# Projections of an attention layer computed feature-major: q and k leave TensorE transposed, the bias is added on VectorE

## The chip, the cores and the metric

The kernel runs on one core of a Trainium2 chip. The metric is the device time of one launch in microseconds. Before the change three runs took 682.51, 686.03 and 685.92 us, median 685.92. The engines are called PE (TensorE, matmul), DVE (VectorE), ACT (ScalarE), POOL (GpSimd) and SP (SyncE, which issues all DMAs here). Each runs its own program in order; they meet by semaphores.

## The reference

Eight sequences of 512 tokens with 256 features, 16 heads of 16. A cross-attention with rotary position, then a feed-forward part with fake quantisation, each behind a gate:

```python
q, k, v = proj(layernorm(x), Wq, bq), proj(ctx, Wk, bk), proj(ctx, Wv, bv)
q = q * cos + rotate_half(q) * sin          # the same for k
attn_w = softmax(q k^T / 4)
x = x + tanh(g0) * ((attn_w v) Wo + bo)
s = sigmoid(clip_x) * max|xn| / 127;  xq = clip(round(xn / s)) * s      # xn = layernorm(x)
h = fake_quant(silu(xq Wg) * (xq Wu), clip_down)     # weights quantised by row
x = x + tanh(g1) * (h Wd)
```

Everything is float32. The scores are computed from three bfloat16 parts of q and k (high, middle, low; six products), so they keep about the accuracy of float32.

## The kernel before

There are three blocks, and all engines leave one together before they enter the next.

**Projection block** (`psA`). It goes through 32 tiles of 128 tokens, four to a batch (a sequence). For a tile, DVE normalises x (`x_normalise`), PE transposes it (`pe_tile`, L256), and multiplies with tokens stationary and weights moving: `v_ps` (L266, 256 columns), the bias of q and k as a bfloat16 matmul of a ones tile with three bias parts (L272, 512 columns), k (L274) and q (L280). DVE rotates q and k out of PSUM with three tensor_tensor (L337 to L339), POOL adds the two halves (L356), PE transposes the result in four pieces (L289), ACT makes the high part from PSUM (L311), DVE the rest from PSUM (L346), ACT the middle part (L305), POOL the low part (L360). The parts go to a scratch tensor in HBM, half a batch at a time (`store`, L369), because the attention wants them by head. `ctx` has two buffers of half a batch, loaded from HBM when the projection of the half before is done (L387). DVE also takes the moments of the next batch (`statistics`, `ln_moments`, L157), POOL the power (-0.5) for them (`ln_power`, L163), and DVE, in the fourth tile of a batch, the largest values of the feed-forward weights (`wmax`, L467), with scales and reciprocals (`winv`) in the last batch. SP loads unit 0 (12 DMAs, `load_unit`, L184) during batch 6 and unit 1 during batch 7, six after each half.

**Attention block** (`psB`). 32 units of four heads. PE computes, two units ahead, the scores by query (`query_scores`, L669), of which DVE takes the row maxima (`maxima`, L880); POOL splits the maxima in two bfloat16 parts (`split_max`, L1004), PE transposes them (`max_transpose`, L694, in step 0 of the unit before the one they serve), ACT copies them (`take_max`), and SP puts them in the q tile as two rows (L628). Then PE computes the scores by key (`scores`, L660), ACT the exponential (L833), PE the weighing of v (`weigh`, L682). A unit has four steps (`kt`), in each 4 maxima on DVE. At its start POOL quantises the gate and up weights with `winv` (L1047, 12 instructions) before batch 0; between batch 0 and batch 1 it makes `woT`, `diag`, the quantised down weights and the integer copy `wfq` (L1050 to L1057).

**Feed-forward block** (`psC`). Not touched by the change.

## Time and profile before

| | us |
|---|---|
| median of three runs | 685.92 |
| the profiled execution | 683.17 |
| its span, first to last instruction | 681.4 |
| PE busy | 613.5 (90%) |
| DVE busy | 569.2 (84%) |
| ACT busy | 432.0 (63%) |
| POOL busy | 249.5 (37%) |
| mean granted clock of PE, share of full | 0.972 |

Busy shares are means over blocks with different limits: the projection block ends at about 143 us, attention at about 580 us. In the rows below, "x4" is a count of instructions merged in one row; a float32 matmul is recorded as two. Times of matmuls include the way through the array, so two that follow each other overlap in the records; the distance between starts is the cost. "[1.96 <-DMA ctx]" is idle time of the engine before the row and what ended it.

### The profile page before, as it was taken

The numbers are of one execution on the slowest core, as the hardware profiler recorded it, in microseconds if no ns is written. First come the engines' busy times: TensorE is split into PE (matmuls) and PEld (weight loads), VectorE is DVE, ScalarE is ACT, GpSimd is POOL, SyncE is SP. The second block draws the span as 40 slices with busy tenths as digits, with TensorE's granted clock in tenths as the row PEclk, the third lists the DMA queues.
The fourth block names the chain that finished last, engine by engine and source line by source line (L and its number), as shares of the span: only waits on it lengthen the run. The fifth ranks groups of instructions, "written<-read, shape, count | busy, mean of one in ns | idle before, by whom it ended". The sixth has DMA issues, their size and how long they took to land. (4 is left out here: it accounts for less than half of the span.)

```text
span 681.4 us, 19413 instructions
## 1 busy us (share of the span) xinstructions
PE 613.5 (90%) x6569; PEld 324.2 (48%) x6574; DVE 569.2 (84%) x1052; ACT 432.0 (63%) x822; POOL 249.5 (37%) x357
## 2 busy tenths in 40 slices
PE   1999998878999999999999999999999997478675
PEld 1777777742544444444444444444444444233254
DVE  7788888878899888888888888988988935489878
ACT  1344544431778776776777777777767774388694
...
GB/s 248 103 176 177 175 180 154 182 140 97 43 68 83 53 69 71 52 66 70 50 69 68 48 68 70 47 66 73 48 67 74 4 1 1 0 1 0 1 62 185
DMA packets 74922, 54.71 MB, mean 80 GB/s; under 512 B 10755, under 2 KB 74371, under 8 KB 74886
## 3 DMA queue, kind: packets, MB, share of 16 engines
...
q14 instruction: 15, 0.12, 0.1%
...
## 5 line engine op out<-in xcount | busy, mean ns | idle before, releaser
L880 DVE TENSOR_REDUCE negm<-mx_ps 128x1 f32<-128x512 f32 x512 | 322.1, 684 | 42.2 <-PE mx_ps L669 37.8
L833 ACT ACTIVATE prob<-st_ps 128x512 f32<-128x512 f32 x512 | 279.2, 600 | 112.7 <-PE st_ps L660 109.9
L669 PE MATMUL mx_ps<-k,q 96*32 96x512 bf16 x2048 | 209.0, 392 | 6.1 <-DVE negm L880 4.9
L660 PE MATMUL st_ps<-q,k 98*32 98x512 bf16 x2048 | 204.0, 385 | 0.2
L682 PE MATMUL pv_ps<-prob,v_u 128*32 128x512 f32 x1024 | 133.4, 592 | 0.3 <-ACT oT L846 0.2
L669 PEld LDWEIGHTS mx_ps<-k,q 96*32 96x32 bf16 x2048 | 56.9, 97 | 103.3 <-DVE negm L880 68.8
L660 PEld LDWEIGHTS st_ps<-q,k 98*32 98x32 bf16 x2048 | 57.9, 96 | 79.6 <-ACT prob L833 34.4
L1004 POOL TENSOR_TENSOR msplit<-negm,onesf 128x16 bf16<-128x16 f32 x32 | 7.1, 221 | 239.2 <-DVE negm L880 234.7
L356 POOL TENSOR_TENSOR qk<-rc,rs 128x512 f32<-128x512 f32 x32 | 40.7, 1271 | 35.0 <-DVE rs L339 35.0
L311 ACT ACTIVATE part<-qkT_ps 128x512 bf16<-128x512 f32 x32 | 19.1, 597 | 42.0 <-PE qkT_ps L289 42.0
L360 POOL TENSOR_TENSOR part<-r,part 128x512 bf16<-128x512 f32 x32 | 38.2, 1194 | 11.9 <-ACT part L305 11.8
L266 PE MATMUL v_ps<-wkv,ctx 128*128 128x256 f32 x128 | 35.5, 402 | 6.4 <-DMA ctx<-in_ctxT 6.4
L682 PEld LDWEIGHTS pv_ps<-prob,v_u 128*32 128x32 f32 x1024 | 32.6, 110 | 18.1 <-issue 1.0
L337 DVE TENSOR_TENSOR rc<-qk_ps,rope_t 128x512 f32<-128x512 f32 x32 | 22.1, 690 | 21.4 <-PE qk_ps L280 18.6
L1247 ACT ACTIVATE wf<-banks,gscale 128x512 f32<-128x512 f32 x44 | 30.0, 696 | 10.6 <-PE banks L1204 4.2
L1394 POOL TENSOR_TENSOR hst<-hq_even,wf 128x512 f32<-128x512 f32 x24 | 30.8, 1302 | 15.5 <-ACT hq_even L1253 15.2
L274 PE MATMUL qk_ps<-wkv,ctx 128*128 128x256 f32 x128 | 33.7, 386 | 0.0
L280 PE MATMUL qk_ps<-wq,xnT 128*128 128x256 f32 x128 | 33.7, 387 | 0.0
L1014 POOL COPY v_u<-V 128x256 f32 (+1 forms) x32 | 12.7, 396 | 49.9 <-PE pv_ps L682 49.8
L1208 PE MATMUL banks<-wfq,wgT 128*128 128x512 bf16 x77 | 23.9, 390 | 4.9 <-ACT wf L1247 3.1
L274 PEld LDWEIGHTS qk_ps<-wkv,ctx 128*128 128x128 f32 x128 | 24.9, 194 | 6.7 <-issue 0.3
L764 PE MATMUL misc_ps<-woT,attnT 128*128 128x256 f32 x112 | 27.8, 391 | 0.0
...
## 6 DMA issues: line engine op xcount, KB each, us to landing
...
q<-mrow SPq DMA_DIRECT2D x64, 4.0 KB, 2.7
...
```

The lines of the kernel that those rows point to most:

```text
L266: last = nc.tensor.matmul(v_ps[r][:, 0:D], ctx[hf][:, c, at:at + P], wkv[:, c, D:2 * D], start=(c == 0), stop=(c == KC - 1))
L274: nc.tensor.matmul(qk_ps[r][:, D:2 * D], ctx[hf][:, c, at:at + P], wkv[:, c, 0:D], start=False, stop=(c == KC - 1), skip_group_check=True)
L280: last = nc.tensor.matmul(qk_ps[r][:, 0:D], xnT[r][:, c, :], wq[:, c, :], start=False, stop=(c == KC - 1), skip_group_check=True)
L356: nc.gpsimd.tensor_tensor(qk[q][:], rc[q][:], rs[q][:], ALU.add).then_inc(roped, 1)
L360: nc.gpsimd.tensor_tensor(parts[j // 2][2][:, :, (j % 2) * P:(j % 2 + 1) * P], r1[i % 2][:], parts[j // 2][1][:, :, (j % 2) * P:(j % 2 + 1 ...
L660: last = nc.tensor.matmul(st_ps[bank(i)][lo:lo + COLS, :], k6[g][:, h, kt * P + lo:kt * P + lo + COLS], q6[g][:, h, :], start=True, stop=True)
L669: last = nc.tensor.matmul(mx_ps[bank(i)][lo:lo + COLS, :], q6[g][0:ROWS, h, qt * P + lo:qt * P + lo + COLS], k6[g][0:ROWS, h, :], start=Tr ...
L682: last = nc.tensor.matmul(pv_ps[32 * h:32 * h + 32, :], v_u[g % 2][:, kt, h, :], prob[kt % 2][:, h, :], start=(kt == 0), stop=(kt == TPB - 1))
L833: nc.scalar.activation(prob[kt % 2][:, h, :], st_ps[bank(HPU * kt + h)][:], ACT.Exp, scale=SCALE).then_inc(exp_done, 1)
L880: nc.vector.tensor_reduce(negm[g % 2][:, h * TPB + qt:h * TPB + qt + 1], mx_ps[bank(TPB * h + qt)][:], op=ALU.max, axis=AX.X, negate=True) ...
L1247: nc.scalar.activation(sil[s % UR], g_ps[s % GR], ACT.Silu, scale=gscale[:, c:c + 1]).then_inc(sil_ready, 1)
L1394: nc.gpsimd.tensor_tensor(hst[:, bass.ds(SLOTS * p + s, 1), :].rearrange("p o t -> p (o t)"), upb[j % UBR], sil[s % UR], ALU.mult).then_in ...
```

## The change

A batch is handled as a whole. PE holds a 128x128 piece of the weights and moves 512 tokens: k (4 matmuls of 512 columns), the 8 transposes of the normalised x, v (tokens stationary, as before), q (4 of 512 columns). q and k come out with features on partitions, in the order "first halves of all heads, second halves of all heads" (the weights are reordered on the host), so a rotation is two scalar_tensor_tensor on DVE for each quarter i (k first half, k second half, q first half, q second half) that add the bias, with a sum or difference after it. The four transposes of q and k and the bias matmul are gone. ACT normalises x instead of DVE. The rotation table grows from 64 KB to 512 KB. The weight maxima go to batch 0 of the attention block, and with them the gate and up quantisation on POOL goes behind batch 0. The SP loop of the projection block is unrolled, and the other engines peel two batches.

```diff
-parts = [[sb(mid, f"part{n}_{i}", [P, 4, 2 * P], BF16) for n in range(3)] for i in range(2)]
+parts = sb(mid, "parts", [P, 4, 3, S], BF16)
-rope_t = sb(mid, "rope_t", [P, TPB, 2, HD])
+work = sb(mid, "work", [P, 4, 2, S])
+bias = sb(mid, "bias", [P, 4])
+cs = sb(mid, "cs", [P, 2, S])
-ctx = [sb(stA, f"ctx{i}", [P, KC, 2 * P]) for i in range(2)]
+ctx = sb(stA, "ctx", [P, KC, S])
+xn = sb(stA, "xn", [P, TPB, D])
+xnT = sb(stA, "xnT", [P, KC, S])
+xT_ps = ps(psA, "xT_ps", [P, KC, S])
+q_ps = ps(psA, "q_ps", [P, 2, S])
+v_ps = ps(psA, "v_ps", [P, TPB, D])
+k_ps = ps(psA, "k_ps", [P, 2, S])
...
+def rope(dve, b, i):
+    h = i % 2
+    dve.wait_ge(qk_ready, 2 * b + i // 2 + 1)
+    if not is_first(b):
+        dve.wait_ge(lo_ready, 4 * (b - 1) + i + 1)
+    src = (k_ps, q_ps)[i // 2]
+    nc.vector.scalar_tensor_tensor(work[:, i, 0, :], src[:, h, :], bias[:, i:i + 1], cs[:, 0, :], ALU.add, ALU.mult)
+    o = i + 1 - 2 * h
+    nc.vector.scalar_tensor_tensor(work[:, i, 1, :], src[:, 1 - h, :], bias[:, o:o + 1], cs[:, 1, :], ALU.add, ALU.mult).then_inc(rot_ready, 1)
+def rope_sum(eng, ns, b, i):
+    eng.wait_ge(rot_ready, 4 * b + i + 1)
+    ns.tensor_tensor(work[:, i, 0, :], work[:, i, 0, :], work[:, i, 1, :], ALU.add if i % 2 else ALU.subtract)\
+        .then_inc(roped_last if i == 3 else roped, 1)
+def hi_part(act, b, i):
+    if i == 3:
+        act.wait_ge(roped_last, b + 1)
+    else:
+        act.wait_ge(roped, 3 * b + i + 1)
+    if not is_first(b):
+        act.wait_ge(stored[i], NSTORE * b)
+    nc.scalar.activation(parts[:, i, 0, :], work[:, i, 0, :], ACT.Copy).then_inc(hi_ready, 1)
+def rest_part(dve, b, i):
+    dve.wait_ge(hi_ready, 4 * b + i + 1)
+    nc.vector.tensor_tensor(work[:, i, 1, :], work[:, i, 0, :], parts[:, i, 0, :], ALU.subtract).then_inc(r1_ready, 1)
+def mid_part(act, b, i):
+    act.wait_ge(r1_ready, 4 * b + i + 1)
+    nc.scalar.activation(parts[:, i, 1, :], work[:, i, 1, :], ACT.Copy).then_inc(mid_ready, 1)
+def lo_part(pool, b, i):
+    pool.wait_ge(mid_ready, 4 * b + i + 1)
+    nc.gpsimd.tensor_tensor(parts[:, i, 2, :], work[:, i, 1, :], parts[:, i, 1, :], ALU.subtract).then_inc(lo_ready, 1)
+scr_rows = scratch.rearrange("n (w c) f t -> n w (c f) t", w=2).rearrange("n w (h e d) t -> n w e h d t", e=2, d=HD // 2)
+def store(sp, b, i):
+    sp.wait_ge(lo_ready, 4 * b + i + 1)
     for n in range(3):
-        sp.dma_start(scr_v[n, :, :, bass.ds(b * S + hf * 2 * P, 2 * P)], parts[hf][n][:]).then_inc(stored[hf], DMA)
+        sp.dma_start(scr_rows[n, 1 - i // 2, i % 2, :, :, bass.ds(b * S, S)], parts[:, i, n, :]).then_inc(stored[i], DMA)
...
+        def load_ctx(b, hf):
+            at = hf * 2 * P
+            if not is_first(b):
+                sp.wait_ge(v_ready, 2 * (b - 1) + hf + 1)
+            sp.dma_start(ctx[:, :, at:at + 2 * P], ctx_v[:, :, bass.ds(b * S + at, 2 * P)]).then_inc(ctx_in[hf], DMA)
         def body(b, unit=None):
+            for i in range(3):
+                store(sp, b - 1, i)
+            if not is_last(b):
+                for hf in range(2):
+                    load_ctx(b + 1, hf)
+            store(sp, b - 1, 3)
+            if unit is not None:
+                load_unit(sp, 0, unit)
+            else:
+                sp.wait_ge(x_in, DMA * (b + 1))
+                load_x(b + 2, x_in)
...
+                pe.wait_ge(ctx_in[hf], DMA * (b + 1))
+            if is_first(b):
+                pe.wait_ge(k_in, DMA)
+            else:
+                pe.wait_ge(rot_ready, 4 * (b - 1) + 2)
+            for m in range(2):
+                for c in range(KC):
+                    last = nc.tensor.matmul(k_ps[:, m, :], wk[:, c, m * P:(m + 1) * P], ctx[:, c, :], start=(c == 0), stop=(c == KC - 1))
+            last.then_inc(qk_ready, 1)
...
+                pe.wait_ge(const_ready, CONSTS)
+            pe.wait_ge(xn_ready, TPB * (b + 1))
+            for c in range(KC):
+                if not is_first(b):
+                    pe.wait_ge(xnT_ready, KC * (b - 1) + c + 1)
+                for t in range(TPB):
+                    last = nc.tensor.transpose(xT_ps[:, c, t * P:(t + 1) * P], xn[:, t, c * P:(c + 1) * P], ident[:])
+                last.then_inc(xT_ready, 1)
+            if is_first(b):
+                pe.wait_ge(v_in, DMA)
+            for j in range(2):
+                if not is_first(b):
+                    pe.wait_ge(v_kept, 2 * (b - 1) + j + 1)
+                for t in (2 * j, 2 * j + 1):
+                    for c in range(KC):
+                        last = nc.tensor.matmul(v_ps[:, t, :], ctx[:, c, t * P:(t + 1) * P], wv[:, c, :], start=(c == 0), stop=(c == KC - 1))
+                last.then_inc(v_ready, 1)
+            if is_first(b):
+                pe.wait_ge(q_in, DMA)
+            else:
+                pe.wait_ge(rot_ready, 4 * (b - 1) + 4)
+            for m in range(2):
+                for c in range(KC):
+                    if m == 0:
+                        pe.wait_ge(xnT_ready, KC * b + c + 1)
+                    last = nc.tensor.matmul(q_ps[:, m, :], wq[:, c, m * P:(m + 1) * P], xnT[:, c, :], start=(c == 0), stop=(c == KC - 1))
+            last.then_inc(qk_ready, 1)
...
+        def normalise(b):
+            act.wait_ge(shift_ready, b + 1)
+            wait_if(act, xT_ready, KC * b)
+            for t in range(TPB):
+                T = TPB * b + t
+                nc.scalar.activation(xn[:, t, :], X[:, bass.ds(T, 1), :].rearrange("p o d -> p (o d)"), ACT.Identity,
+                                     bias=shift[:, bass.ds(T, 1)], scale=rstd[:, bass.ds(T, 1)]).then_inc(xn_ready, 1)
         def body(b):
+            if not is_first(b):
+                for i in (0, 1):
+                    mid_part(act, b - 1, i)
+                for i in (2, 3):
+                    hi_part(act, b - 1, i)
+            for c in range(KC):
+                act.wait_ge(xT_ready, KC * b + c + 1)
+                if c == 0:
+                    wait_if(act, qk_ready, 2 * b)
+                nc.scalar.activation(xnT[:, c, :], xT_ps[:, c, :], ACT.Copy).then_inc(xnT_ready, 1)
+            if not is_first(b):
+                for i in (2, 3):
+                    mid_part(act, b - 1, i)
+            for j in range(2):
+                act.wait_ge(v_ready, 2 * b + j + 1)
+                nc.scalar.activation(V[:, bass.ds(TPB * b + 2 * j, 2), :], v_ps[:, 2 * j:2 * j + 2, :], ACT.Copy).then_inc(v_kept, 1)
+            for i in (0, 1):
+                hi_part(act, b, i)
+            if not is_last(b):
+                normalise(b + 1)
+        normalise(0)
+        over_batches(act, body, B, True, 2)
...
+            ahead = not is_last(b)
+            if not is_first(b):
+                for i in (2, 3):
+                    rope(dve, b - 1, i)
+            if ahead:
+                dve.wait_ge(x_in, DMA * (b + 1))
+                statistics(b + 1, (0, 1))
+            if not is_first(b):
+                rope_sum(dve, nc.vector, b - 1, 3)
+            if ahead:
+                statistics(b + 1, (2, 3))
+            if not is_first(b):
+                for i in (2, 3):
+                    rest_part(dve, b - 1, i)
+            for i in (0, 1):
+                rope(dve, b, i)
+            if ahead:
+                dve.wait_ge(ln_ready[0], b + 1)
+                ln_moments(nc.vector, dve, 0, b + 1)
+            for i in (0, 1):
+                rest_part(dve, b, i)
 ...
+        def scale_and_shift(b):
+            ln_power(pool, 0, b)
+            pool.wait_ge(ln_ready[0], b + 1)
+            cols = bass.ds(TPB * b, TPB)
+            nc.gpsimd.tensor_tensor(shift[:, cols], negmean[:, cols], rstd[:, cols], ALU.mult).then_inc(shift_ready, 1)
         def body(b):
+            if not is_first(b):
+                lo_part(pool, b - 1, 0)
+                rope_sum(pool, nc.gpsimd, b - 1, 2)
+                lo_part(pool, b - 1, 1)
+                lo_part(pool, b - 1, 2)
+            rope_sum(pool, nc.gpsimd, b, 0)
+            if not is_first(b):
+                lo_part(pool, b - 1, 3)
+            rope_sum(pool, nc.gpsimd, b, 1)
+            if not is_last(b):
+                scale_and_shift(b + 1)
...
+                    if is_first(b):
+                        weight_maxima(TPB * g + kt)
...
+        def weight_maxima(n):
+            if n == 0:
+                dve.wait_ge(late_in, 11 * DMA)
+            if n < 12:
+                nc.vector.tensor_reduce(wmax[:, n:n + 1], wf[:, n, :], op=ALU.max, axis=AX.X, apply_absolute_value=True).then_inc(w_step, 1)
+            elif n < 12 + KC:
+                i = n - 12
+                nc.vector.tensor_reduce(wmax[:, WD + i:WD + i + 1], wd[:, i, 0:INNER], op=ALU.max, axis=AX.X,
+                                        apply_absolute_value=True).then_inc(w_step, 1)
+            elif n == 14:
+                dve.wait_ge(w_step, 2 * NIC + KC)
+                for lo, hi in ((0, 2 * NIC), (WD, NROW)):
+                    last = nc.vector.tensor_scalar(wscale[:, lo:hi], wmax[:, lo:hi], 1.0 / QMAX, None, ALU.mult)
+                last.then_inc(w_step, 1)
+                dve.wait_ge(tanh_ready, 2)
+                nc.vector.tensor_scalar(clips[:], clipe[:], 1.0, QMAX, ALU.add, ALU.mult).then_inc(clip_step, 1)
+            else:
+                dve.wait_ge(w_step, 2 * NIC + KC + 1)
+                for lo, hi in ((0, 2 * NIC), (WD, NROW)):
+                    last = nc.vector.reciprocal(winv[:, lo:hi], wscale[:, lo:hi])
+                last.then_inc(w_step, 1)
+                dve.wait_ge(clip_step, 1)
+                nc.vector.reciprocal(clips[:], clips[:])
...
+        pool.wait_ge(bo_ready, 2)
+        body(0)
+        pool.wait_ge(w_step, 2 * NIC + KC + 2)
         for i in range(2 * NIC):
             nc.gpsimd.tensor_scalar(wf[:, i, :], wf[:, i, :], winv[:, i:i + 1], MAGIC, ALU.mult, ALU.add)
-        pool.wait_ge(bo_ready, 2)
-        body(0)
```

At the start SP loads, in order, wk, both halves of ctx, x of batch 0, the bias, the rotation table, wv, wq, x of batch 1, the gates, ctx and x of later batches, and the feed-forward weights. In the attention block the parts of batch 7 that are left are made between the first maxima (DVE: `rope` 2 and 3, four maxima, `rope_sum` 3, four maxima, `rest_part` 2 and 3).

## Rows read from the trace of the kernel before

**Rows 1.** Timeline of SP's DMA issues: start, us, engine, line.
```profile
48.89 1.53 SPq L369 DMA_DIRECT2D qk_parts<-part  x3
...
110.55 1.53 SPq L369 DMA_DIRECT2D qk_parts<-part  x3
...
112.13 3.40 SPq L184 DMA_DIRECT2D k<-qk_parts  x6
...
115.58 0.43 SPq L387 DMA_DIRECT2D ctx<-in_ctxT  x1
```

**Rows 2.** Timeline of PE, one tile, and one wait for ctx.
```profile
111.40 0.38 PE L272 MATMUL qk_ps<-b_parts,onesb 96*128 96x512 bf16 x1
...
111.62 1.03 PE L274 MATMUL qk_ps<-wkv,ctx 128*128 128x256 f32 x4
...
113.35 0.60 PE L289 MATMUL qkT_ps<-ident,qk 128*128 128x128 f32 x4
...
113.78 0.38 PE L256 MATMUL xT_ps<-ident,xn 128*128 128x128 f32 x2
...
114.87 0.38 PE L272 MATMUL qk_ps<-b_parts,onesb 96*128 96x512 bf16 x1
...
119.60 1.13 PE L266 MATMUL v_ps<-wkv,ctx 128*128 128x256 f32 x4 [1.96 <-DMA ctx<-in_ctxT]
```

**Rows 3.** Busy time by stretch: us; PE, PEld, DVE, ACT, POOL; granted clock.
```profile
180.00:191.00 11.00, 11.00 (x165) 5.76 (x165) 10.00 (x17) 8.76 (x18) 0.84 (x4) 1.00 0.31 76
```

**Rows 4.** Groups by form, first 115 us: busy us, mean ns, idle before.
```profile
L356 POOL TENSOR_TENSOR qk<-rc,rs 128x512 f32<-128x512 f32 x25 | 31.8, 1272 | 28.0 <-DVE rs L339 28.0
...
L360 POOL TENSOR_TENSOR part<-r,part 128x512 bf16<-128x512 f32 x23 | 27.7, 1203 | 4.2 <-ACT part L305 4.2
...
L346 DVE TENSOR_TENSOR r<-qkT_ps,part 128x512 f32<-128x512 f32 x24 | 16.4, 682 | 0.2 <-issue 0.2
...
L467 DVE TENSOR_REDUCE wmax<-wf x5 | 3.4, 678 | 0.0
...
L163 POOL TENSOR_TENSOR rstd<-ln_tmp,ln_const 128x4 f32 x5 | 5.6, 1116 | 1.9 <-DVE ln_tmp L157 1.9
```

**Rows 5.** Groups by form after 590 us (feed-forward part).
```profile
L1320 DVE SCALAR_TENSOR_TENSOR hst<-banks,gscale,wf 128x512 f32<-128x512 f32 x10 | 7.5, 746 | 8.8 <-ACT wf L1247 8.7
```

**Rows 6.** Timeline of ACT in the attention part.
```profile
217.95 2.73 ACT L833 ACTIVATE prob<-st_ps 128x512 f32<-128x512 f32 x5
```

**Rows 7.** One line's instructions: duration ns min/median/max.
```profile
L157 DVE TENSOR_TENSOR ln_tmp<-stats x21: 150/153/1149, 26.1 to 119.7; 128x4 f32 x18, 128x4 f32<-128x4 f32 x3
```

**Rows 8.** Timeline: both engines in one such place.
```profile
118.45 1.26 POOL L356 TENSOR_TENSOR qk<-rc,rs 128x512 f32<-128x512 f32 x1 [0.96 <-DVE rs L339]
...
118.88 1.00 DVE L157 TENSOR_TENSOR ln_tmp<-stats 128x4 f32 x3
```

**Rows 9.** Timeline of the first microseconds: POOL's memset of the k tiles.
```profile
8.01 7.61 POOL L534 MEMSET k<- 2x2048 bf16 x4
```

**Rows 10.** Timeline across the end of the projection block.
```profile
143.87 0.69 DVE L337 TENSOR_TENSOR rc<-qk_ps,rope_t 128x512 f32<-128x512 f32 x1 [2.71 <-PEq L373]
```

**Rows 11.** Timeline of POOL in the attention part, first batch.
```profile
158.14 5.46 POOL L1047 TENSOR_SCALAR wf<-wf,winv 128x256 f32<-128x256 f32 x12
...
204.78 1.04 POOL L1050 TENSOR_TENSOR woT<-wo_raw,tanhg 128x512 f32<-128x512 f32 x1
...
208.38 4.03 POOL L1057 TENSOR_SCALAR wfq<-wf 128x4608 bf16<-128x4608 f32 x1
...
213.57 0.22 POOL L1004 TENSOR_TENSOR msplit<-negm,onesf 128x16 bf16<-128x16 f32 x1 [1.16 <-DVE negm L880]
```

**Rows 12.** Timeline of PE there.
```profile
215.88 0.23 PE L694 MATMUL misc_ps<-identb,msplit 128*32 128x128 bf16 x1
```

**Rows 13.** Busy time by stretch, end of attention, same columns as rows 3.
```profile
580.00:583.00 3.00, 0.00 (x0) 0.00 (x0) 2.00 (x5) 0.00 (x0) 0.93 (x1) 0.83 0.00 0
...
589.00:592.00 3.00, 2.77 (x7) 1.06 (x7) 0.00 (x0) 1.18 (x2) 0.00 (x0) 0.50 0.00 0
```

More of the change, by code:

```diff
@@ L55, with over_batches @@
 DMA = 16
-def over_batches(eng, body, count, peel_last):
-    body(0)
-    with eng.Fori(1, count - 1 if peel_last else count) as b:
+def over_batches(eng, body, count, peel_last, peel_first=1):
+    for b in range(peel_first):
+        body(b)
+    with eng.Fori(peel_first, count - 1 if peel_last else count) as b:
         body(b)
@@ L102, in build @@
         mean = sb(top, "mean", [P, NT])
+        negmean = sb(top, "negmean", [P, NT])
+        shift = sb(top, "shift", [P, NT])
         rstd = sb(top, "rstd", [P, NT])
@@ L141, in ln_moments @@
             cols = bass.ds(TPB * b, TPB)
-            half, quarter, per, eps, _ = (ln_const[:, i, :] for i in range(len(LN_CONST)))
+            half, quarter, per, eps, neg_half = (ln_const[:, i, :] for i in range(len(LN_CONST)))
             levels = [[(tmp[0][:], stats[:, cols, 1], stats[:, cols, 4], ALU.add),
@@ L154, in ln_moments @@
                 if done:
-                    eng.wait_ge(step, LN_STEPS * b + done)
+                    eng.wait_ge(step, LN_STEPS[k] * b + done)
                 for out, x0, x1, op in level:
@@ L240, in build @@
         lo_ready = sem("lo_ready")
[L241 removed]
+        stored = [sem(f"stored{i}") for i in range(4)]
         NSTORE = 3 * DMA
[L244 to L290 removed]
@@ L373, in build @@
+        CONSTS = 5
         with nc.Block() as block:
@@ L396, in _ @@
+                sp.dma_start(wk[:], a["wkT"].rearrange("(c p) n -> p c n", p=P)).then_inc(k_in, DMA)
+                for hf in range(2):
+                    load_ctx(0, hf)
                 load_x(0, x0_in)
-                sp.wait_ge(b_zero, 1)
-                sp.dma_start(b_raw[0:65:32, :], a["bqk"].partition_broadcast(3)).then_inc(bias_in, DMA)
-                sp.dma_start(wkv[:], a["wkvT"].rearrange("(c p) n -> p c n", p=P)).then_inc(kv_in, DMA)
-                sp.dma_start(ctx[0][:], ctx_v[:, :, 0:2 * P]).then_inc(ctx_in[0], DMA)
+                sp.dma_start(bias[:], a["bkq"]).then_inc(bias_in, DMA)
@@ L405, in _ @@
                 sp.dma_start(gates[:], a["gates"].partition_broadcast(P)).then_inc(gate_in, DMA)
-                body(0)
+                for hf in range(2):
+                    load_ctx(1, hf)
                 sp.wait_ge(x_in, DMA)
@@ L419, in _ @@
                 sp.dma_start(bv_col[:], a["bv_col"]).then_inc(late_in, DMA)
-                with sp.Fori(1, B - 2) as b:
+                for b in range(1, B - 2):
                     body(b)
-                for hf in range(2):
-                    sp.wait_ge(stored[hf], NSTORE)
+                for i in range(4):
+                    sp.wait_ge(stored[i], NSTORE)
                 body(B - 2, 0)
@@ L489, in _ @@
+                    for i in (0, 1):
[5 more added lines that the diff above has]
+                        rest_part(dve, b, i)
                 dve.wait_ge(ln_const_ready, len(LN_CONST))
                 dve.wait_ge(x0_in, DMA)
-                for i in range(2):
-                    statistics(0, i)
+                statistics(0, range(TPB))
@@ L512, in _ @@
-                body(B - 1)
+                dve.wait_ge(bias_in, 2 * DMA)
+                over_batches(dve, body, B, True, 2)
             @block.gpsimd
             def _(pool):
-                def body(b):
-                    for i in range(TPB):
-                        pool_tile(pool, TPB * b + i, i, 0)
-                        if i == 2 and not is_last(b):
-                            ln_power(pool, 0, b + 1)
-                nc.gpsimd.memset(b_raw[:], 0.0).then_inc(b_zero, 1)
+                def scale_and_shift(b):
[3 more added lines that the diff above has]
+                    nc.gpsimd.tensor_tensor(shift[:, cols], negmean[:, cols], rstd[:, cols], ALU.mult).then_inc(shift_ready, 1)
```

277 lines of the change are left out of this document (48 added, 229 removed).

## The prediction, made before the changed kernel was run

> **What bounds the kernel now.** I read the slices first (TensorE is full from about 170 us to 570 us and ragged before), then the timeline of each stage, then the groups by form for durations.
>
> The projection block (to about 143 us). SP stores the first half of a batch at 48.89 and four batches later at 110.55 [rows 1]: 61.66 / 4 = 15.4 us a batch. On PE a tile takes 114.87 - 111.40 = 3.47 us without a gap, four tiles 13.9 us, and the rest is the wait for `ctx`: issued at 115.58, used at 119.60, PE idle 1.96 us [rows 1, 2]. So this block is TensorE plus a late reload. The other engines have room: POOL has 1.27 + 1.20 us a tile plus 1.1 us a batch [rows 4], 11.0 us of 15.4.
>
> The attention block. A unit takes about 11 us in its first batch, PE 11.00 of 11.00 us, DVE 10.00 [rows 3]. PE is the bound with DVE close behind. A PE stall there is not given back.
>
> **TensorE in the change.** q, k and v keep their products: what moves doubles to 512 columns and the instructions halve. Four 256-column matmuls take 1.73 / 2 = 0.87 us (113.35 - 111.62 covers k and q) [rows 2], so a 512-column one takes 0.43 x 2 = 0.87 us. Gone are the bias matmul, 0.22 us, and four transposes of q and k, 113.78 - 113.35 = 0.43 us a tile [rows 2]. A batch then needs 4 x (3.47 - 0.65) = 11.3 us of PE. Were PE the bound with no reload wait, the block would win 4 us a batch.
>
> **What becomes the bound instead.** The work per batch is now a ring through POOL and ACT, both in program order: POOL `sum(b,1)` -> POOL power and shift of b+1 -> ACT four normalisations -> ACT `mid(b,0)` -> POOL `lo(b,0)` -> `sum(b,2)` -> ACT `hi 2`, `hi 3`, two `xnT`, `mid 2` -> POOL `lo(b,2)` -> `sum(b+1,0)` -> `lo(b,3)` -> `sum(b+1,1)`. Priced:
> - POOL: 3 sums x 1.27 = 3.8; 3 lo x 1.20 = 3.6; power 1.1 and a 0.2 us shift = 1.3 [rows 4]; 8.7.
> - ACT: back to back, 512 columns cost (2.73 - 0.60) / 4 = 0.53 us each, the last 0.60 [rows 6]. Four 256-column normalisations are not in the trace: between 1.1 (half of 0.53 each) and 2.1 (0.53 each); I take 1.5, since each has a fixed part. `mid(b,0)` 0.6; hi, hi, xnT, xnT 2.1; `mid 2` 0.6. Together 4.8.
> - Handoffs between engines, five at 0.1 us: 0.5.
> That is 14.0 us. `lo(b,1)` lies beside ACT's five, at no cost.
>
> DVE per batch: eight rotations (a DVE scalar_tensor_tensor of this shape takes 0.746 us [rows 5], about 0.66 back to back) 5.3, five subtractions or sums at 0.6 to 0.68 [rows 4] 3.2, statistics 1.4, moments about 1: 11 us. It is under the ring by amount, but not by the port. A DVE tensor_tensor of 128x4 on SBUF alone takes 0.153 us, and up to 1.149 [rows 7]; one such case starts at 118.88 while POOL's sum runs from 118.45 to 119.71, and three of them need 1.00 us [rows 8]. DVE waits for POOL's instruction. Before, the large DVE operations of this block read one operand from PSUM (`qk_ps`, `qkT_ps`). Now `rest_part` x4 and `rope_sum 3` read both from SBUF, so they wait for POOL, or POOL for them. On the ring: `rope_sum 3` gets in between `lo(b,0)` and `sum(b,2)`, +0.6; and the ten moment operations get in one at a time between `sum 0`, `lo 3` and `sum 1`, so the power starts about 1.1 us later. 14.0 + 1.7 = 15.7 us a batch. Bounds: 13.6 if the port is used with no gap (POOL 8.6, DVE 5 x 0.68 and 1.6 of moments), 16.5 if each rest also waits.
>
> The Trainium skill has a rule for it (page "SBUF — State Buffer", section "Who interferes with whom"): a DVE instruction with two SBUF inputs contends with a GpSimd instruction that reads SBUF, and the second one blocks for the whole of the first. Rows 7 and 8 agree with 1.149 against 0.153 us. Without that rule the ring alone would hold, 14.0 us, and the sum below would end 10 us lower.
>
> The reload of `ctx` is one buffer now: SP issues it behind the stores of `lo 2`. From `lo(b-1,2)`: three stores 1.5, two issues 0.8, landing 3.6: 6.0 us to `k(b+1)` [rows 1, 2]. By way of k, the transposes, `xnT`, `mid 2`, `lo 2` this loop closes in 13.2 us, under the ring. PE then has one gap of 4.4 us a batch.
>
> **Start and end of the block.** The x load stands behind 0.75 MB of weights and ctx, so POOL's memset (8.01, 7.61 us [rows 9]) starts about 2.8 us later (1 to 4) and `sum(0,0)` at 18.5. One pass of the ring with less waiting, 13.3 us, puts `lo(0,2)` at 31.8. Six periods: 31.8 + 6 x 15.7 = 126.0. SP is last then: `lo(6,3)` 2.5 us on, its stores 1.5, and then twelve loads of unit 1, 2 x 3.40 = 6.8 [rows 1], that were spread between stores before: 137.0, with the other engines done 6 us earlier. All engines leave the block together (DVE sat 2.71 us for PE's end [rows 10]), so DVE starts the attention block at 137.4 instead of 143.87 [rows 10]: **-6.4**.
>
> **Attention block.**
> - Left over on DVE at its start, between maxima that set the pace: four rotations 2.6, one sum 0.6, two rests 1.2 = 4.4 us, against 2.5 before (0.6 and 2 x 0.33 for a rotation, 2 x 0.6 for rests): **+2.0** (1 to 3).
> - Weight maxima, one in each of 16 steps of batch 0: 12 at about 0.33, two of 704 columns at 0.8, scales and reciprocals 0.7 (0.678 us for 512 columns [rows 4]): 6.3 us. DVE's room is 1.0 us in each of two units and 0.7 in two [rows 3]: 3.4. The rest comes mostly in unit 3: **+2.2** (0 to 4).
> - POOL quantises the weights later. Before, 12 tensor_scalar (5.46 us) ran before batch 0; then from 204.78 to 208.38 + 4.03 = 212.41 the rest, 7.63 us, ending 1.16 us before the last maxima of unit 3 let it make `split_max(1,1)` at 213.57 [rows 11]. PE wants that at 215.88, in step 0 of unit 4 [rows 12], and waits in order: scores, maxima and weighing of unit 4 are queued behind it. Now POOL must first wait for `winv`, which DVE makes in the last step of unit 3 (213.57 + 0.4 on this clock), and then does 5.46 + 7.63 = 13.1 us and the split (0.5) before PE goes on: 213.97 + 13.1 + 0.55 = 227.6, against 215.88: **+11.8**. It happens once. The bounds are 10 and 13.
> - PE's clock. After 577 PE was idle and the granted clock fell within 580 to 583 (mean 0.83) with no PE work in it; dense work then ran at 0.50, which is 1.2 GHz, for 3 us [rows 13]. An idle stretch of 11.8 us gets the same; 3 to 6 us at half speed cost 1.5 to 3: **+2.2**.
> The feed-forward part is untouched: 0.
>
> **Sum.** -6.4 + 2.0 + 2.2 + 11.8 + 2.2 = +11.8. The profiled execution took 683.17 us (span 681.4 and 1.8 around it): 695.0. The median of the runs, 685.92, lies 2.75 above it, so I give 697 us.
>
> **Rivals.**
> 1. The port has no bite: the ring holds at 14.0. Six periods 10.2 and the start 1.5 less: 697 - 12 = 685. For it: DVE has slack in which a wait may vanish. Against: the port's total is 13.6 of 14.0. Chance 0.18.
> 2. Faster. The ring does not close, because ACT runs ahead and POOL's gaps fall beside it, and the reload loop sets 13.2 us or less: 6 x 2.5 + 1.5 = 16.5 less, 681. It decides once normalisation, `mid 0` and the four ACT operations take under 4 us together. For it: ACT has only about 9 us of work. Against: the order of its program. Chance 0.13.
> 3. The weight work does not stall PE, all else as forecast: 697 - 14 = 683. Only if PE lagged POOL by a unit; rows 11 and 12 show 2.3 us. Chance 0.07.
> 4. PE's 4.4 us gap in each batch lowers its clock in the projection block. The reload loop has k at half speed in it: 13.2 + 3.4 = 16.6 a batch, 6 x 0.9 = 5 more: 702 or above. For it: rows 13. Against: PE is over 70% busy in each period. Chance 0.12.
> The forecast has 0.50, and 691 to 702 for its own range.
>
> **How the numbers follow.** A measurement of this kernel tells 0.5%, 3.4 us, from no change. Faster takes rival 2 (0.13) and the low edge of rival 3 (0.02): 0.15. Same: rival 1 and most of rival 3: 0.22. Slower: the forecast and rival 4: 0.63. The range leaves out rival 2 and the far end of rival 4: 682 to 706.
>
> **What would show it.** Stores of one batch to the next: 15.7 us apart (14.0 for rival 1, 13.2 for rival 2). `rest_part` and `rope_sum` on DVE at 0.68 us at best and over 1 us where POOL runs. The last rows of the projection block: only SP issuing for 6 us. The maxima of unit 1 ending about 4 us earlier than before. `msplit` of unit (1,1) more than 13 us after the last maxima of unit 3, PE idle 11 to 12 us before its transpose, and granted clock 0.5 behind it. The prediction is wrong if PE is not idle there, or if the block ends before 125 us.

## The result and the profile after

The changed kernel takes 695.79 us (median of 4 runs, 693.82 to 696.59) against 685.65 us (682.51 to 686.03) for the kernel before on the same chip: ratio 1.0153, 95% interval 1.0131 to 1.0175, so 9.0 to 12.0 us slower. The forecast was 697 us. The profiled executions are 13.0 us apart (spans 694.4 and 681.4), the medians 10.1. One profiled execution can lie 2 to 3 us from its median, as that of before does (683.17 against 685.65).

In what follows "(b,i)" is quarter i of batch b, in the attention block unit g of batch b. A "rest" is what is left when a part is subtracted: `rest_part` on DVE, `lo_part` on POOL.

The page of the changed kernel, its span and its first engine:

```profile
span 694.4 us, 18601 instructions
...
PE 603.4 (87%) x6281; PEld 282.2 (41%) x6286; DVE 560.7 (81%) x1003; ACT 441.9 (64%) x822; POOL 242.1 (35%) x355
```

The timeline of the projection block and of its end (start, us, engine, line; in brackets the idle time before and what ended it), answering to [rows 1, 2, 10]:

```profile
71.32 6.38 PE L366 MATMUL k_ps<-ctx,wk 128*128 128x512 f32 x8 [5.02 <-DMA ctx<-in_ctxT]
...
87.12 3.69 PE L366 MATMUL k_ps<-ctx,wk 128*128 128x512 f32 x8 [1.66 <-DMA ctx<-in_ctxT]
...
71.11 2.07 ACT L409 ACTIVATE xn<-X,shift,rstd 128x256 f32 x4 [2.27 <-POOL shift L482]
...
73.78 1.16 POOL L282 TENSOR_TENSOR parts<-work,parts 128x512 bf16<-128x512 f32 x1 [3.01 <-ACT parts L277]
...
69.59 0.59 SPq L302 DMA_DIRECT2D X<-in_x  x1
...
74.93 0.75 DVE L443 BATCH_NORM_STATS2 stats<-X  x2 [2.17 <-DMA X<-in_x]
...
43.10 7.07 SPq L290 DMA_DIRECT2D qk_parts<-parts  x9
...
123.56 8.87 SPq L290 DMA_DIRECT2D qk_parts<-parts  x12
132.47 2.94 SPq L189 DMA_DIRECT2D k<-qk_parts  x6
135.45 2.77 SPq L189 DMA_DIRECT2D q<-qk_parts  x6
...
132.93 0.69 DVE L272 TENSOR_TENSOR work<-work,parts 128x512 f32<-128x512 f32 x1 [1.81 <-ACT parts L267]
138.74 0.75 DVE L249 SCALAR_TENSOR_TENSOR work<-q_ps,bias,cs 128x512 f32<-128x512 f32 x1 [5.12 <-PEq L294]
...
138.66 1.47 PE L643 MATMUL mx_ps<-k,q 96*32 96x512 bf16 x12 [8.15 <-PEq L294]
```

Three waits are to be seen in each batch: PE for `ctx`, POOL 3.01 us for ACT's `mid` parts (ACT normalises first, from 71.11 to 73.18), and DVE 2.17 us for `X`, which SP issued at 69.59 behind stores and `ctx`. The first stores of a batch stand 16.1 us apart (the first at 43.10, the sixth at 123.56). At the end SP alone works from 133.6 to 138.2, on unit 1's loads.

Groups by form of the first 139 us (busy us, mean ns, idle before), answering to [rows 4]:

```profile
L282 POOL TENSOR_TENSOR parts<-work,parts 128x512 bf16<-128x512 f32 x28 | 33.8, 1209 | 31.9 <-ACT parts L277 31.9
L256 POOL TENSOR_TENSOR work<-work 128x512 f32<-128x512 f32 x23 | 31.0, 1348 | 0.3
...
L272 DVE TENSOR_TENSOR work<-work,parts 128x512 f32<-128x512 f32 x30 | 22.1, 770 | 13.7 <-ACT parts L267 13.6
...
L256 DVE TENSOR_TENSOR work<-work 128x512 f32<-128x512 f32 x7 | 7.6, 1087 | 0.0
...
L443 DVE BATCH_NORM_STATS2 stats<-X x20 | 7.5, 415 | 8.4 <-DMA X<-in_x 8.4
```

The attention block, first batch, answering to [rows 11, 12]:

```profile
165.10 0.22 POOL L1012 TENSOR_TENSOR msplit<-negm,onesf 128x16 bf16<-128x16 f32 x1 [9.86 <-DVE bo_b L974]
...
212.65 5.47 POOL L1058 TENSOR_SCALAR wf<-wf,winv 128x256 f32<-128x256 f32 x12 [10.16 <-DVE winv L946]
...
221.69 4.03 POOL L1066 TENSOR_SCALAR wfq<-wf 128x4608 bf16<-128x4608 f32 x1
225.68 0.22 POOL L1012 TENSOR_TENSOR msplit<-negm,onesf 128x16 bf16<-128x16 f32 x1
...
226.33 0.28 PE L668 MATMUL misc_ps<-identb,msplit 128*32 128x128 bf16 x1 [11.38 <-POOL msplit L1014]
226.44 0.62 PE L634 MATMUL st_ps<-q,k 98*32 98x512 bf16 x4
...
230.52 0.39 PE L634 MATMUL st_ps<-q,k 98*32 98x512 bf16 x4
...
230.96 0.39 PE L634 MATMUL st_ps<-q,k 98*32 98x512 bf16 x4
...
233.13 0.39 PE L634 MATMUL st_ps<-q,k 98*32 98x512 bf16 x4
...
237.17 0.22 POOL L1012 TENSOR_TENSOR msplit<-negm,onesf 128x16 bf16<-128x16 f32 x1 [10.64 <-DVE negm L856]
```

Two of the same splits in the kernel before:

```profile
168.03 0.22 POOL L1004 TENSOR_TENSOR msplit<-negm,onesf 128x16 bf16<-128x16 f32 x1 [4.42 <-DVE bo_b L968]
...
224.82 0.22 POOL L1004 TENSOR_TENSOR msplit<-negm,onesf 128x16 bf16<-128x16 f32 x1 [8.72 <-DVE negm L880]
```

Busy time by stretch, the columns of [rows 3, 13]:

```profile
220.00:226.00 6.00, 0.00 (x0) 0.00 (x0) 0.00 (x0) 0.00 (x0) 5.83 (x5) 0.51 0.09 10
226.00:229.00 3.00, 2.67 (x29) 1.24 (x33) 1.31 (x2) 1.53 (x4) 0.54 (x2) 0.50 0.00 0
229.00:232.00 3.00, 3.00 (x40) 1.04 (x36) 1.58 (x4) 1.44 (x4) 0.00 (x0) 0.77 0.02 3
```

The split of unit (0,1)'s maxima stood at 168.03 before: the change is 2.9 us ahead at 165.10. The split of unit (1,2) stood at 224.82 and stands at 237.17, 12.35 us behind. So the stretch between them loses 15.3 us, and nothing of it comes back: 13.0 us at the end. In it PE waits 11.38 us for POOL's quantisation, then works at the clock of 0.50: six groups of score matmuls and a weighing take 4.08 us (226.44 to 230.52), the next that are alike 2.17 us (230.96 to 233.13), so the low clock costs 1.9 us there.

### The profile page after: what moved, and what is told of

Read it like the earlier page. It is cut to its first block and busy times, and to the rows that moved or that the text cites. A ratio compares the mean times of both kernels' runs of the same rounds, so it can differ in the third digit from the quotient of the medians.

```text
span 694.4 us, 18601 instructions
## 1 busy us (share of the span) xinstructions
PE 603.4 (87%) x6281; PEld 282.2 (41%) x6286; DVE 560.7 (81%) x1003; ACT 441.9 (64%) x822; POOL 242.1 (35%) x355
## 5 line engine op out<-in xcount | busy, mean ns | idle before, releaser
L643 PE MATMUL mx_ps<-k,q 96*32 96x512 bf16 x2048 | 211.4, 400 | 13.8 <-PEq L294 8.1
L366 PE MATMUL k_ps<-ctx,wk 128*128 128x512 f32 x64 | 38.7, 760 | 27.4 <-DMA ctx<-in_ctxT 27.4
L282 POOL TENSOR_TENSOR parts<-work,parts 128x512 bf16<-128x512 f32 x32 | 38.4, 1202 | 37.2 <-ACT parts L277 37.2
L267 ACT ACTIVATE parts<-work 128x512 bf16<-128x512 f32 x32 | 19.4, 626 | 37.7 <-POOL work L256 35.3
L656 PEld LDWEIGHTS pv_ps<-prob,v_u 128*32 128x32 f32 x1024 | 32.2, 110 | 18.8 <-issue 1.3
L1403 POOL TENSOR_TENSOR hst<-hq_even,wf 128x512 f32<-128x512 f32 x24 | 30.7, 1294 | 15.5 <-ACT hq_even L1262 15.2
L366 PEld LDWEIGHTS k_ps<-ctx,wk 128*128 128x128 f32 x64 | 15.0, 247 | 50.1 <-issue 50.1
L272 DVE TENSOR_TENSOR work<-work,parts 128x512 f32<-128x512 f32 x32 | 23.3, 764 | 13.7 <-ACT parts L267 13.6
L256 POOL TENSOR_TENSOR work<-work 128x512 f32<-128x512 f32 x24 | 32.2, 1345 | 0.3
L409 ACT ACTIVATE xn<-X,shift,rstd 128x256 f32 (+1 forms) x32 | 16.6, 589 | 24.7 <-POOL shift L482 24.7
L397 PE MATMUL q_ps<-xnT,wq 128*128 128x512 f32 x64 | 28.9, 594 | 0.5 <-ACT xnT L422 0.5
L386 PE MATMUL v_ps<-wv,ctx 128*128 128x256 f32 x128 | 29.0, 379 | 0.0
L1277 ACT ACTIVATE wf<-hst,ainv 128x1024 int16<-128x1024 f32 (+1 forms) x24 | 23.8, 1066 | 6.2 <-DVE ainv L1297 4.3
```

The costliest lines, as they stand in the source:

```text
L256: ns.tensor_tensor(work[:, i, 0, :], work[:, i, 0, :], work[:, i, 1, :], ALU.add if i % 2 else ALU.subtract)\
L282: nc.gpsimd.tensor_tensor(parts[:, i, 2, :], work[:, i, 1, :], parts[:, i, 1, :], ALU.subtract).then_inc(lo_ready, 1)
L366: last = nc.tensor.matmul(k_ps[:, m, :], wk[:, c, m * P:(m + 1) * P], ctx[:, c, :], start=(c == 0), stop=(c == KC - 1))
L386: last = nc.tensor.matmul(v_ps[:, t, :], ctx[:, c, t * P:(t + 1) * P], wv[:, c, :], start=(c == 0), stop=(c == KC - 1))
L397: last = nc.tensor.matmul(q_ps[:, m, :], wq[:, c, m * P:(m + 1) * P], xnT[:, c, :], start=(c == 0), stop=(c == KC - 1))
L643: last = nc.tensor.matmul(mx_ps[bank(i)][lo:lo + COLS, :], q6[g][0:ROWS, h, qt * P + lo:qt * P + lo + COLS], k6[g][0:ROWS, h, :], start=Tr ...
```

## The experiments

All ratios are to the kernel before, run on the same chip. Differences from the changed kernel are differences of ratios (its own is 1.0153) times 685.5 us; each carries the uncertainty of the changed kernel's ratio, 1.5 us, besides that of the run. The edits are shown in short form.

**1. The quantisation apart.** The 13 us of POOL work behind batch 0 are spread over the ends of batches 0, 1 and 2.

```
 body(0)
+woT ...
+body(1)
 wait maxima; 12 x tensor_scalar(wf ...)
-woT ...
 diag ...; wd ...
+body(2)
 wfq ...
-body(1)
-Fori(2, B - 1)
+Fori(3, B - 1)
```

> The changed kernel with POOL's weight work spread: woT after batch 0, the twelve gate and up quantisations with the down ones and diag after batch 1, the integer copy wfq after batch 2; each piece (1 us, 8 us, 4 us) is shorter than the 9 to 10 us in which POOL waits for maxima. Theory: the PE stall of 11.4 us in unit 4 and the half clock behind it (about 2 us) go, nothing else moves: 695.8 - 13.5 = 682.3 us, PE idle under 1 us before the transpose of the maxima in unit 4, granted clock 1.0 throughout. Rival (the pause only gathers waits that PE would meet later in the batch, since DVE is near its limit with the weight maxima in it): 4 us or less is won, 692 us or more.

682.08 us (680.27 to 683.35, 8 runs), 0.9959 [0.9946, 0.9973]: 13.3 us less, as much as the 11.4 us of the wait and the 1.9 us of the low clock together. Busy time by stretch in this run:

```profile
205.00:235.00 30.00, 30.00 (x418) 11.90 (x414) 27.73 (x53) 23.26 (x46) 1.68 (x6) 1.00 0.33 68
```

PE is full at full clock where it stood 11.4 us. The place of POOL's work was the loss, not its amount: the three pieces fit into POOL's idle time.

**2. The same in the kernel before.** Only the weight work moves, as in the change; the projections stay row-major.

```
-weights' maxima in the projection batches (DVE)
-12 x tensor_scalar(wf ...) ahead of the first attention batch (POOL)
+weight_maxima(step) in the steps of attention batch 0
 body(0)
+12 x tensor_scalar(wf ...)
```

> The kernel before with one part of the change alone: weight maxima in batch 0 of the attention block, the gate and up quantisation on POOL behind batch 0. Its projection block is the old one without the maxima. Theory: the attention part of the sum by itself, maxima on DVE +1.7, stall +11.4, clock +2, and nothing from the projection block since DVE had room there: 685.7 + 15 = 700.7 us. Rival (the old DVE order in the projection block was tight, and the maxima gone from it win 2 us or more): 698 us or less; if the stall needs the new projections, 687 us.

701.06 us (700.08 to 702.25, 4 runs), 1.0246 [1.022, 1.0272]. POOL's timeline shows the same stall, and so does PE's empty stretch:

```profile
217.09 5.47 POOL L1053 TENSOR_SCALAR wf<-wf,winv 128x256 f32<-128x256 f32 x12 [10.16 <-DVE winv L947]
...
230.12 0.22 POOL L1007 TENSOR_TENSOR msplit<-negm,onesf 128x16 bf16<-128x16 f32 x1
```

```profile
222.00:228.00 6.00, 0.00 (x0) 0.00 (x0) 0.00 (x0) 0.00 (x0) 5.91 (x8) 0.50 0.13 31
```

The weight work moved costs 16.9 us; the whole change 10.5. The rest of it, the projections themselves, gained 6.4 us by the ratios (uncertain by 2.3) and 4.6 us by the spans of the two profiles (699.0 and 694.4). The prediction had 4.4 for it: 6.4 at the block's end less 2.0 for DVE's leftovers.

**3. The same, spread**: run 2 with the edit of run 1.

> The kernel before with the weights' maxima and quantisation moved into the attention (701.06 us alone) and the quantisation then spread over the ends of POOL's batches 0, 1 and 2, as in the first run on the changed kernel (-13.3 us there). Theory (POOL's stall behind batch 0 is the same in both kernels, and independent of the projections): 701.1 - 13.3 = 687.8 us (686 to 690), 2 us over the kernel before, the price of the maxima on DVE. Rival (the row-major projections gained from having the weights' work out of their way, and this shows once the stall is gone): under 684 us.

686.87 us (685.09 to 689.12, 10 runs), 1.0036 [1.0016, 1.0056]. Run 1's 13.3 us are 14.4 us here; what is left of moving the weight work is 0.36%, 2.5 us, near the maxima's price. The rival (under 684) is out.

**4. Unit 1's load later.** SP's last batch doesn't issue the twelve loads of unit 1; they come first in the attention block.

```
-body(B - 1, 1)
+body(B - 1, no unit)
 ...
+load_unit(sp, 0, 1)
 load_unit(sp, 0, 2)
```

> The changed kernel with the twelve loads of unit 1 moved from the end of SP's projection program to the head of its attention program. Theory (all engines leave the block together and SP is last): the pause between PE's last projection matmul and its first score shrinks from 8.2 us to about 2.5 us, and since unit 1 is asked for 9 us after the block starts, that is won in full: 695.8 - 5.5 = 690.3 us. Rival (the loads only move: the stores of batch 7 and the first maxima rows queue behind them on SP, the first scores by key wait): 1 us or less is won, 695 us.

690.63 us (690.26 to 690.99, 4 runs), 1.0092 [1.007, 1.0114]: 4.2 us less. PE's first operation in the attention block:

```profile
133.42 0.83 PE L644 MATMUL mx_ps<-k,q 96*32 96x512 bf16 x12 [2.03 <-PEq L294]
```

It starts 5.2 us earlier and its idle time is 2.03 us instead of 8.15. The loads had held all engines at the block's end.

**5. One input.** `rest_part` and DVE's `rope_sum` are replaced by two `bn_stats` over the same columns, which read one SBUF tile and take about as long. The subtraction and that sum are left out. The replacements also write less, 6 columns for each 256 they read, so the run doesn't separate reading from writing.

```
-nc.vector.tensor_tensor(work[:, i, 1, :], work[:, i, 0, :], parts[:, i, 0, :], ALU.subtract)
+for h in range(2):
+    nc.vector.bn_stats(dst[:, h * D:h * D + 6], src[:, h * D:(h + 1) * D])
```

> The changed kernel with rest_part and DVE's rope_sum replaced by two statistics instructions over the same 512 columns, which read one operand from SBUF and take about the same time on DVE (0.66 against 0.60 us). It leaves out the subtraction for the middle and low parts and the sum of quarter 3. Port theory: POOL's instructions no longer grow (its sums now 1.35 us in the mean, 1.27 alone) and DVE's no longer wait; a batch takes 0.8 to 1.5 us less than 16.1, the block ends 6 to 10 us earlier: 686 to 690 us. Only the small moment operations still read two operands from SBUF. Rival (the waits at the port fall beside the wait for the x load, which ends later): a batch takes 15.8 to 16.1 us, 694 to 696 us.

692.48 us (691.7 to 692.89, 4 runs), 1.0115 [1.0093, 1.0138]: 2.6 us less (uncertain by 2.2), between the two theories. The timeline (DVE, then SP's stores):

```profile
57.30 0.75 DVE L451 BATCH_NORM_STATS2 stats<-X  x2 [1.51 <-DMA X<-in_x]
...
63.55 1.64 DVE L162 TENSOR_TENSOR ln_tmp<-stats 128x4 f32 x3
...
42.03 7.36 SPq L298 DMA_DIRECT2D qk_parts<-parts  x9
...
119.41 1.19 SPq L298 DMA_DIRECT2D qk_parts<-parts  x2
```

The period falls from 16.1 to (119.41 - 42.03) / 5 = 15.5 us. The moments, which still have two SBUF inputs, still wait (1.64 us for three operations of 128x4), and DVE still waits for `X`. So of the 1.7 us that the prediction gave to the port, taking the large operations off it won 0.6; something else stood at 15.5, and may hide more.

**6 to 8. Two orders.** Run 6: ACT makes `mid(b,0)` and `mid(b,1)` before it normalises batch b+1. Run 7: SP issues the load of x at the head of its batch. Run 8: both.

```
 hi_part(act, b, 0), hi_part(act, b, 1)
+mid_part(act, b, 0), mid_part(act, b, 1)
 normalise(b + 1)
-(next batch) mid_part(act, b, 0), mid_part(act, b, 1)
 SP, body(b):
+load_x(b + 2)
 store(b - 1, 0 to 2); load_ctx(b + 1, 0 and 1); store(b - 1, 3)
-load_x(b + 2)
```

> One edit on the changed kernel: ACT does the second part (mid) of k's two halves of batch b before it normalises batch b+1, instead of behind it. In the changed kernel POOL stands idle 3.01 us a batch for these, which stand behind four normalisations of 0.59 us. Theory (the period of 16.1 us is held by two loops: the context load behind POOL's third rest, and the load of x, which stands behind it on SP and for which DVE's statistics wait 1.9 us a batch): the idle time of POOL goes from 3.0 to under 1 us, but the normalisation comes later, the x load stays where it is and the period falls only to some 15.6 us; 692.5 us (690 to 695), 0.995 of the changed kernel. Rival (ACT's order alone holds the period): the period falls by the whole idle time to 13.5 us or so, over six batches 15 us, 681 us.

> One edit on the changed kernel: SP issues the load of x at the head of its batch instead of behind the four stores and the two context loads. Theory (two loops, as in the run beside it): DVE's wait of 1.9 us a batch for x goes, the loop through POOL's third rest stays, lengthened by one issue of 0.5 us or shortened a little because DVE's rest parts come earlier; period 15.2 to 15.6 us, 691.5 us (689 to 695). Rival (the x load alone holds the period): 13.5 us a batch, 681 us.

> The two edits of the runs beside it together (ACT's mid parts before the normalisation, x loaded first). Theory (two loops of nearly one length): together they give clearly more than the sum of the two alone, the period falls to 13.2 to 13.8 us (POOL's ten operations of 1.2 to 1.35 us and its power are then the bound), six batches times 2.5 us: 681 us (677 to 685). Rival (the period is held by the work of DVE and POOL on one port, not by these orders): no more than 1 us a batch, 690 us.

- Run 6: 688.69 us (687.12 to 689.98, 6 runs), 1.0055 [1.0037, 1.0073]: 6.7 us less, twice what was expected.
- Run 7: 695.48 us (694.48 to 696.56, 4 runs), 1.0148 [1.0123, 1.0174]: nothing that the medians can show. In its profile PE's attention starts at 137.13 instead of 138.66.
- Run 8: 686.36 us (685.24 to 688.13, 10 runs), 1.0021 [1.0009, 1.0032]: 9.0 us less, not 15.

The orders aren't equal. In run 7 the wait for `X` is gone and POOL waits as long for `mid` as before (3.02 us at 73.45); DVE then waits for `hi`, and a period is 15.65 us (POOL's first rests at 73.45 and 89.10). So ACT's order held the period, and the x load was the next limit: in run 6 a period is 14.7 us (POOL's first rests at 73.47 and 88.19), and DVE waits 2.08 us of it for `X`. The theory, that the two together give clearly more than their sum, isn't shown: 9.0 against 7.0 us, with an uncertainty of 2.7. Run 8 is 2.3 us (uncertain by 1.5) faster than run 6 by the ratios; by the profiles their spans are 684.8 and 685.4, and the attention block starts at the same time (PE, run 6, then run 8):

```profile
128.32 1.47 PE L643 MATMUL mx_ps<-k,q 96*32 96x512 bf16 x12 [7.08 <-PEq L294]
```

```profile
128.37 1.47 PE L643 MATMUL mx_ps<-k,q 96*32 96x512 bf16 x12 [6.96 <-PEq L294]
```

PE's, DVE's and SP's timeline in run 8, DVE without idle time from 59.4 to 79:

```profile
68.21 3.69 PE L366 MATMUL k_ps<-ctx,wk 128*128 128x512 f32 x8 [2.46 <-DVE work L251]
...
70.03 1.64 DVE L256 TENSOR_TENSOR work<-work 128x512 f32<-128x512 f32 x1
...
76.08 1.51 DVE L162 TENSOR_TENSOR ln_tmp<-stats 128x4 f32 x3
...
125.16 2.77 SPq L189 DMA_DIRECT2D q<-qk_parts  x6
```

The period is 13.8 us in the middle, as forecast (POOL's first rests at 74.06 and 87.83). The 15 us were missed because they counted six periods; batches 0 and 1 are set by the first loads (`k` of batch 2 starts at 39.59 in the changed kernel and 38.55 in run 8), and from there to batch 7's the time falls from 79.5 to 71.4 us, 8.1 us. Run 6 alone is nearly there: its `k` of batch 2 starts at 37.12 and that of batch 7 at 109.79, against 109.96 in run 8. At the end both wait for SP, which issues context, stores and the loads of units 0 and 1 with hardly a gap from 104.9 to 127.9 us. And in the middle DVE is now the bound, with its waits for POOL: 1.64 us for a sum of 0.68.

**9. Context loads a store earlier**, with the two orders.

```
-store(b - 1, 0 to 2); load_ctx(b + 1, 0 and 1); store(b - 1, 3)
+store(b - 1, 0 and 1); load_ctx(b + 1, 0 and 1); store(b - 1, 2 and 3)
```

> The changed kernel with the two orders of the last runs (mid parts before the normalisation, x loaded first) and one edit more: SP issues the context loads behind the second store of a batch instead of the third. Against the run with the two orders alone (686.4 us, whose steady period of 13.8 us shows DVE with no idle time, but whose first and last batches still wait 1.4 to 4.6 us for the context). Theory (the 5 us by which the combined kernel, at 663.8, lies under the sum of its parts, 668.8, are this edit's, in the batches where DVE isn't full and before the end of the block): 681.5 us (679.5 to 684). Rival (they come from the three stretches meeting differently, this edit is hidden): 686 us.

684.61 us (682.11 to 689.35, 10 runs), 1.0007 [0.9984, 1.003]: between the theory and the rival, and it can't be told from run 8. PE at the block's end:

```profile
106.29 3.60 PE L367 MATMUL k_ps<-ctx,wk 128*128 128x512 f32 x8
...
127.00 1.47 PE L644 MATMUL mx_ps<-k,q 96*32 96x512 bf16 x12 [8.47 <-PEq L294]
```

Batch 7's `k` starts 3.7 us earlier than in run 8, PE's attention only 1.4 us: SP issues with hardly a gap from 103.5 to 126.6 us, unit 1's loads last, and takes the rest. That this edit is worth more with that of run 4 is likely, but no pair of runs has it alone.

**10. All together**: the edits of runs 1, 4, 8 and 9.

> All that the runs point to, on the changed kernel: the weights' quantisation spread over the ends of POOL's batches 0, 1 and 2 of the attention (-13.3 us measured against the changed kernel), unit 1's load moved behind the projections' end (-4.2 measured), ACT's mid parts before the normalisation and x loaded first (-15 forecast), and the context loads issued after the second store of a batch instead of the third (-0 to -4). Theory (the parts are in three stretches and add up): 695.8 - 13.3 - 4.2 - 16 = 662 us (656 to 668). Rival (the faster projections don't reach the end, because something else, the waits for the stores of the last batch or the loads of units 0 and 2, sets the start of the attention): 695.8 - 17.5 = 678 us.

663.80 us (662.36 to 666.38, 4 runs), 0.9683 [0.9658, 0.9708]: 3.2% faster than the kernel before, 32 us faster than the change as it was. PE's last `k` and its start in the attention block:

```profile
107.27 3.60 PE L367 MATMUL k_ps<-ctx,wk 128*128 128x512 f32 x8
...
122.41 1.47 PE L645 MATMUL mx_ps<-k,q 96*32 96x512 bf16 x12 [2.88 <-PEq L294]
```

The attention starts at 122.41, 16.3 us before the changed kernel's. The parts add up: runs 1, 4 and 8 alone give 13.3 + 4.2 + 9.0 = 26.5 us by the ratios and 12.8 + 5.7 + 9.6 = 28.1 us by the spans of their profiles; all together give 32.2 and 29.8. The second pair leaves 1.7 us for the context loads and for chance; the first pair's 5.7 has an uncertainty of some 4 us, from five ratios, and isn't located further.

**11. Matmuls in PE's gap**, on the changed kernel.

```
 pe.wait_ge(rot_ready, ...)
+for n in range(8):
+    nc.tensor.matmul(k_ps[:, 0, 0:D], wk[:, 0, 0:P], wk[:, 1, :], start=True, stop=True)
 pe.wait_ge(ctx_in ...)
```

> The changed kernel; PE does eight matmuls of 128x256 (wk against wk, into k's accumulator, which the first real matmul overwrites) before it waits for the context of a batch. They fill 1.8 us at full clock of a gap of 2.3 to 5.0 us. It asks whether the k matmuls at the low clock (5.19, 6.38 and 6.12 us instead of 3.70 in batches 2, 4 and 6) cost time at the end. Theory (the period is held by the load of x, the statistics, POOL's rests and SP, a loop that has no matmul in it): k's matmuls come near 3.7 us, but the time falls by 3 us at the most: 694.5 us (692.5 to 696.5). Rival (the matmuls are in the loop): 1.5 + 2.7 + 2.4 = 6.6 us less, 689.5 us.

695.19 us (693.41 to 695.84, 4 runs), 1.0154 [1.0129, 1.0179]: no change. Timeline of PE and the stretch of six batches:

```profile
65.52 3.62 PE L363 MATMUL k_ps<-wk 128*128 128x256 f32 x16
69.70 3.67 PE L368 MATMUL k_ps<-ctx,wk 128*128 128x512 f32 x8 [0.57 <-DMA ctx<-in_ctxT]
```

```profile
38.00:120.00 82.00, 78.94 (x296) 52.07 (x295) 70.48 (x140) 45.14 (x85) 51.56 (x47) 1.00 0.58 165
```

The eight took 3.62 us, twice the estimate. In batch 1 they held `k` up (25.02 against 22.38); from batch 2 on no `k` started more than 0.1 us later than without them (69.70 against 71.32 in batch 4). Each `k` takes 3.6 to 3.7 us and the granted clock is 1.00 over the whole stretch, as in the kernel before; it is 0.90 in the changed kernel. In the profiled execution the attention starts at 137.21 instead of 138.66; the medians show nothing of it, with an uncertainty of 2.3 us. The low clock of `k` is worth 1.5 us by the profiles.

**12. The fourth sum on POOL**, on the combined kernel.

```
-rope_sum(dve, nc.vector, b - 1, 3)
 rope_sum(pool, nc.gpsimd, b - 1, 2)
+rope_sum(pool, nc.gpsimd, b - 1, 3)
```

> The combined kernel (663.8 us) with the rotation's fourth sum moved from DVE to POOL, behind its third. In the combined kernel DVE has no idle time in a period of 13.8 us, this sum takes 1.64 us of it (0.68 of work, the rest a wait while POOL works), and POOL stands idle 3.7 us a batch. Theory (DVE is the bound now, and the waits of its two-input operations for POOL are part of it): DVE's list falls to 12.2, POOL's rises by 1.27 us; the period falls to some 12.9 us, over five batches 4.5 us less: 659.5 us (657 to 662). Rival (POOL, with its longer chain up to the third rest, becomes late, or the 128x4 operations of DVE wait as much longer as the sum did): 664 to 667 us.

662.95 us (661.61 to 665.35, 4 runs), 0.9687 [0.9654, 0.972]: it can't be told from run 10; the rival's case. Timeline:

```profile
83.50 2.56 DVE L272 TENSOR_TENSOR work<-work,parts 128x512 f32<-128x512 f32 x2
...
81.44 2.51 POOL L256 TENSOR_TENSOR work<-work 128x512 f32<-128x512 f32 x2
```

Two rests on DVE, 1.27 us in run 10, take 2.56 beside POOL's sums. Most of the wait moved from the sum to the rests: over the block DVE's seven sums of 9.8 us are gone, and its thirty rests take 27.4 us instead of 20.7. DVE's two-input work and POOL's take turns, so shifting an operation from one to the other gains little: by the profiles the period falls from 13.8 to 13.5 us and the attention starts at 120.11 instead of 122.41, which the medians can't show. The Trainium skill has the taking of turns (page "SBUF — State Buffer", section "Who interferes with whom"): a DVE instruction with two SBUF inputs contends with a GpSimd instruction that reads SBUF, and the lock is exclusive. The 2.56 against 1.27 us agree.

## Why the prediction was right, step by step

The time, 697 against 695.79 us, and the mechanism held; its terms came within 1.3 us of what was measured. (Two slips of its sums cost less than 1 us: 126.0 + 2.5 + 1.5 + 6.8 is 136.8, not 137.0, and 695.0 + 2.75 is 697.7, given as 697.) By the profiled executions, where +11.8 was forecast and +13.0 came:

- PE's 11.3 us a batch: right. From one `k` at 54.84 to the end of `q` at about 66.2.
- The period, 15.7 us: 16.1 between first stores, 15.9 over the six from `lo(0,2)` to `lo(6,2)`. The ring through POOL and ACT does hold it (run 6), and alone it is 15.65 us (run 7), but its terms were off. Four normalisations take 2.07 us, not 1.5; taking the large operations off the port won 0.6 of the 1.7 us (run 5), and what the rest is made of no run shows. Missed altogether was the load of x: it stands on SP behind the stores and `ctx`, and DVE waits 1.3 to 2.2 us a batch for it. It was a limit of its own, about 1 us behind the ring (14.7 us in run 6). So the right total of the ring was partly luck.
- `lo(0,2)` at 31.8: 33.1. `lo(6,2)` at 126.0: 128.2.
- The end of the block, held by SP's twelve loads: right in kind (run 4), 138.7 instead of 137.4. The block won 5.1 us instead of 6.4. SP worked alone for 4.6 us, not 6.
- DVE's leftovers, +2.0: 2.2 (the block ends 5.1 us ahead, the split of unit (0,1) 2.9).
- Weight maxima, +2.2: about 1.8, from that split to the end of unit 3's last maxima (45.4 us before, 47.3 after), and 2.5 us with all else removed (run 3). The prediction's own terms, 6.3 us of work in 3.4 us of room, leave 2.9.
- POOL's quantisation, +11.8: PE stood 11.38 us [rows 11, 12]. Run 1 takes it away, run 2 gives it to the kernel before.
- The clock, +2.2: 0.50 for 3 us and 0.77 for the next 3. What is left of the 12.35 us at the split of unit (1,2) is 12.35 + 2.9 - 1.8 - 11.4 = 2.1 us, and the matmuls behind the stall show 1.9 of it. No run has the stall without the clock.
- The feed-forward block, 0: its first products start 12.45 us later than before (601.68 against 589.23), so 0.5 us of the 13.0 comes in it. No run looks into that.

Of the rivals, the fourth was seen and hardly counted: `k` ran slowly in batches 2, 4 and 6 (5.19, 6.38 and 6.12 us), but PE is not in the ring that closes last, and run 11 finds 1.5 us in it by the profiles. The first and the second needed a period of 14.0 or 13.2; the ring stands at 15.65, and only with both orders changed did a period come to 13.8. The third, no stall, is out.
